# First context pair ahead of the loops' other work, and VectorE's last-stage weight work behind the row statistics

## The chip, the cores and the metric

One core of a Trainium2 chip runs the whole program. The time is device microseconds of one execution; three runs of the kernel before are shown, and one more execution was taken by the profiler. Engine names are the profile's: PE is TensorE, DVE VectorE, ACT ScalarE, POOL GpSimd, SP SyncE (which only issues transfers here).

## The reference

Two layers work on x of 64 batches x 128 rows x 256 columns in float32, each with cross attention to a context of the same shape and then a mixture of experts, all gated by tanh:

```python
x = x + tanh(g_xattn[0]) * xattn0(layernorm(x), ctx)      # 16 heads of 16, W_qkv, W_proj, b_proj
x = x + tanh(g_ffn[0])   * ffn0(layernorm(x))             # top 1 of 8 experts, capacity 1.5, 256-1024-256, gelu
x = x + tanh(g_xattn[1]) * xattn1(layernorm(x), ctx, ctx) # 16 heads of 16, wq, wk, wv, wo
x = x + tanh(g_ffn[1])   * ffn1(layernorm(x))             # top 2 of 4 experts, 256-256-256, two layer norms inside
```

In ffn0 every token is put into a slot of its expert's buffer (its place is the count of tokens before it with the same choice), the experts run over the slots, and each token reads its slot back, weighted with its softmax value.

## The kernel before

The work has four stages in a row. **The first attention loop** (n = 0) takes one batch of 128 rows per step through a pipeline that reaches over some 18 steps; step s works on batch s + 4 at one end (x_in is loaded) and on batch s - 12 at the other (its rows are scattered into the experts' slots in DRAM). **The expert stage** runs 39 groups of 256 slots through two layers, with weights split into a high and a low half. **The second attention loop** (n = 1) runs the same steps for layer 1; its input is x1 plus the weighted expert output, which an indirect DMA on GpSimd's queue gathers per batch (y_in, line 698, five steps ahead), and VectorE adds (x2 or "rows", line 1543, four steps ahead). **The last stage** (fstep) starts inside the tail of that loop.

Each engine has its own program, written out by hand: `step(s)` of that engine is a list of `if` blocks, each for one operation on its own batch, and the engine does them in the order of the text. Engines meet through counting semaphores. The attention loops are written out whole, with steps from -5 (LEAD) to 64 + 13 or 64 + 6, so "step 7" below is one definite place in each engine's program. The names that matter:

- Start of a loop. SyncE loads the weights (line 492), then in its steps x_in of batch s + 4 (line 529) and, in odd steps, the context c_t of the pair s + 3, s + 4 (line 536); for the first pair this is step -3, behind two x_in loads. In step -1 it waits until all four high and low halves of the key and value weights are made (s_wv, line 554) and loads the projection weights wp over w_vp (line 555). ScalarE makes wk_hi and wv_hi ahead of its steps (lines 818, 819), VectorE wv_lo and wk_lo (lines 1425, 1426), and TensorE waits for all four (line 1068).
- Context. ScalarE copies c_t to c_hi (line 861) and GpSimd subtracts to c_lo (line 730), both two steps ahead; TensorE makes the keys of a pair in one go (line 1148, 12 products; for the first pair in step -1), ScalarE copies them to k_in (line 869), and the values come a step later (line 1158). The values need wv_hi and wv_lo, the keys wk_hi and wk_lo.
- Rows. VectorE takes the statistics (bn_stats, bn_aggr, lines 1497, 1501, batch s + 3), GpSimd makes rstd (lines 675, 677), VectorE xh (line 1442), TensorE turns it (line 1216), ScalarE copies it to x_t (line 837), TensorE makes the query (line 1241).
- Scores. GpSimd masks k_in and q_in to km_r and qm (line 668); TensorE makes the scores of batch s - 1 (line 1098), VectorE their maximum nmax (line 1434, the first thing in its step, 2.29 us), TensorE turns it (line 1168), VectorE spreads it (nmax_x, line 1476), TensorE makes the final scores (lines 1075, 1081), ScalarE the exponential (line 889), TensorE the product with the values (line 1127). Then VectorE divides (rden, o_n, lines 1508, 1510), TensorE turns o_n in the next step (line 1111), ScalarE copies it (o_t, o_hi), GpSimd makes o_lo (line 714), TensorE projects (line 1227), and VectorE adds the residual (x1, line 1536).
- Weights of the last stage. SyncE loads them in step 2 of the second loop (line 490, 3 MB and some small ones). VectorE prepares them in 20 of the steps 7 to 42 (lines 1585 to 1652), at the end of its step, in pieces of mostly 1024 columns.
- Slots. In every fourth step of the first loop VectorE turns counts into slots (lines 1451 to 1470, for the chunk of four batches that begins with s - 12); GpSimd's scatters (line 740, batch s - 12) wait for them. The first group of the experts waits for the last scatter.
- End of the experts. SyncE stores the last block (line 590) and waits until it and the one before have landed (line 594) before it goes into the second loop; GpSimd waits for the same (line 753).

Of the kernel before, what the change touches and what calls it, by code (L numbers as in the profile page):

```python
# [5 lines left out]
P = 128  # L6
# [106 lines left out]
def flamingo_gated(nc, x, ctx_in, consts, gates, wq, wk, wv, wp, b_proj, router, w1_0, b1_0, w2_0, b2_0,  # L113
# [24 lines left out]
    QK_AT, PROB_AT = 11022, 15630  # L138
# [8 lines left out]
    with es:  # L147
# [58 lines left out]

        w_q = sb("w_q", [P, C, D])
# [23 lines left out]
        slot_in = psb("slot_in", [P, 4, 1], I32)  # L231
# [223 lines left out]
        def _(sp):  # L455
# [53 lines left out]
            for n in range(2):  # L509
# [8 lines left out]
                def step(s):  # L518
                    if n == 0 and s.known and s.off == FIRST_WEIGHTS:
                        weights(At(0, 0))  # L520
                    if n == 1 and s.known and s.off == LAST_WEIGHTS:
                        layer1_weights()
                    b = s + 4
# [6 lines left out]
                    e = s + 3  # L530
                    if e.off % 2 == 0 and e.within(B):
                        if (e - 3).begun:
                            sp.wait_ge(y["c_lo_done"].of(e - 3), y["c_lo_done"].at(e - 3))
                        for t in range(2):
                            b = e + t
                            sp.dma_start(c_t[:, e.off // 2 % 2, :, t, :], row(ctx_in, b).rearrange("p (c k) -> p c k", c=C))\
                                .then_inc(y["c_came"].of(b), 16)
# [22 lines left out]
                if n == 0:  # L560
# [32 lines left out]
                    for g in (NH - 2, NH - 1):  # L593
                        sp.wait_ge(z["eo_stored"].of(At(0, g)), z["eo_stored"].at(At(0, g)))
# [7 lines left out]
        def _(pool):  # L602
# [61 lines left out]
            for n in range(2):  # L664
# [14 lines left out]
                def step(s):  # L679
# [5 lines left out]
                    b = s - 5  # L685
                    if n == 0 and b.within(B):
                        if (b - 1).begun:
                            pool.wait_ge(y["xh2_done"].of(b - 1), y["xh2_done"].at(b - 1))
                        rstd(y["n2_stats"], mv2, rs2, y["n2_rstd"], b)
                    b = s + 5  # L690
                    if n == 1 and b.within(B):
# [17 lines left out]
                    b = s - 4  # L709
                    if b.within(B):  # L710
                        pool.wait_ge(y["o_t_done"].of(b), y["o_t_done"].at(b))
                        if (b - 2).begun:
                            pool.wait_ge(y["pr_done"].of(b - 2), y["pr_done"].at(b - 2))
                        nc.gpsimd.tensor_tensor(o_lo[:, b.parity], o_t[:, b.parity], o_hi[:, b.parity], ALU.subtract)\
                            .then_inc(y["o_lo_done"].sem, 1)
# [1111 lines left out]
```

## Time and profile before

| what | value |
|---|---|
| three runs | 2114.24, 2115.59, 2116.48 us (median 2115.59) |
| profiled execution | 2114.74 us |
| its span (first to last instruction) | 2112.6 us |
| mean granted TensorE clock | 0.985 |
| PE / DVE / ACT / POOL busy | 2019.0 / 1760.6 / 1479.2 / 1201.8 us |
| attention 0, experts, attention 1 and last stage | about 0 to 559, 559 to 1024, 1024 to 2113 us |

The profiled execution's own time is 2.1 us over its span. Busy shares are averages over stages with different limits; what one place is worth has to be read from the rows of that place. In the rows, times are microseconds from the start of the span; a row gives the start, the duration, the engine, the line, the operation, output<-inputs, and in square brackets how long the engine had been idle before it and what released it.

### The profile page before, as it was taken

Reading aid. Unit: us, or ns where it says so; the run is one execution under the profiler, and the core shown is the slowest. Engines: PE = TensorE matmul, PEld = TensorE weight load, DVE = VectorE, ACT = ScalarE, POOL = GpSimd, SP = SyncE. Lnnn points to the kernel's source line nnn. Section 1 sums busy time; section 2 is a strip of 40 time slices with the busy share of each in tenths; the row PEclk is TensorE's granted clock in tenths of the full one; section 3 lists DMA queues with packets and bytes.
Section 4 is the critical chain, followed back from the end, with each engine's and each line's share of the span. In section 5 each row is a group of like instructions: output and inputs, shape, how many; then the busy total and the mean of one; then the engine's idle time right before and its main releaser. Section 6 shows DMA issues by size and latency. Waiting matters only on the chain.

```text
span 2112.6 us, 57359 instructions
## 1 busy us (share of the span) xinstructions
PE 2019.0 (96%) x19532; PEld 1772.0 (84%) x19532; DVE 1760.6 (83%) x4918; ACT 1479.2 (70%) x3172; POOL 1201.8 (57%) x1736
## 2 busy tenths in 40 slices
PE   6999999999699999999699999999999999999997
PEld 5878888887599999999578887888788888888885
DVE  5888888888588888888588888888589999999996
ACT  4766666666487878787366666666578888888885
POOL 5778888887200000000377777777357777777776
PEclk9999999999799999999899999999999999999998
DMA  7565222221466666666422222222101100011000
GB/s 243 171 198 169 69 72 64 69 74 38 162 244 222 245 228 239 229 235 238 153 59 76 69 74 69 74 69 77 39 24 31 31 31 30 31 31 30 30 27 18
DMA packets 168047, 226.09 MB, mean 107 GB/s; under 512 B 20454, under 2 KB 152170, under 8 KB 157420
## 3 DMA queue, kind: packets, MB, share of 16 engines
q1 hardware_dynamic: 161644, 205.99, 29.5%
q0 software_dynamic: 6144, 16.79, 2.6%
q8 instruction: 145, 2.38, 0.5%
q14 instruction: 114, 0.93, 0.2%
HBM read 153.77 MB, written 68.94 MB: 105 GB/s over the span
## 4 chain that ended last, share of the span: by engine, by line
PE 87%; DVE 5%; issue 3%; DMA 2%; POOL 1%; ACT 1%; SPq 0%; POOLq 0%; ACTq 0%; DVEq 0%
PE ps L1281 11%; PE ps L1297 11%; PE ps L1041 10%; PE ps L1000 8%; PE ps L1081 5%; PE ps L1127 5%; PE ps L1241 4%; PE ps L1227 4%; PE ps L1148 4%; PE ps L1158 3%; PE ps L1181 3%; DVE nmax L1434 3%; PE ps L1060 3%; PE ps L1075 2%; PE ps L1098 2%
## 5 line engine op out<-in xcount | busy, mean ns | idle before, releaser
L1434 DVE TENSOR_REDUCE nmax<-ps 128x16 f32<-128x2048 f32 x128 | 292.8, 2287 | 32.6 <-PE ps L1098 32.2
L889 ACT ACTIVATE prob_t<-ps 128x2048 f32<-128x2048 f32 x128 | 240.8, 1881 | 102.4 <-PE ps L1081 102.4
L694 POOL COPY slot_in<-slot_all 128x1 int32<-128x1 int32 x64 | 13.3, 207 | 473.4 <-DMA eo_d<-eo 473.4
L1041 PE MATMUL ps<-w2f,a_t 128*128 128x256 f32 x1024 | 231.7, 379 | 0.3 <-ACT a_t L811 0.3
L1281 PE MATMUL ps<-xgt_hi,w_hl 128*128 128x256 f32 x1248 | 230.6, 283 | 1.0 <-DVE xgt_lo L1701 1.0
L1297 PE MATMUL ps<-w_hl,hid_hi 128*128 128x256 f32 x1248 | 226.9, 284 | 0.0
L1041 PEld LDWEIGHTS ps<-w2f,a_t 128*128 128x128 f32 x1024 | 189.6, 190 | 23.8 <-ACT a_t L811 0.6
L961 ACT ACTIVATE hid<-ps,b_in 128x256 f32<-128x256 f32 x312 | 145.8, 468 | 83.5 <-PE ps L1281 68.0
L1281 PEld LDWEIGHTS ps<-xgt_hi,w_hl 128*128 128x128 f32 x1248 | 196.0, 190 | 1.4 <-issue 1.4
L811 ACT ACTIVATE a_t<-ps,be_in,g_in 128x128 f32<-128x128 f32 x512 | 185.6, 469 | 12.3 <-PE ps L1060 11.4
L1297 PEld LDWEIGHTS ps<-w_hl,hid_hi 128*128 128x128 f32 x1248 | 191.5, 188 | 0.0
L1692 DVE TENSOR_TENSOR w_hl<-w_raw,w_hl 128x1024 fp32r<-128x1024 f32 x152 | 176.0, 1220 | 15.7 <-ACT w_hl L937 15.7
L668 POOL TENSOR_TENSOR km_r<-k_in,cst 128x512 fp32r<-128x512 f32 x128 | 134.4, 1050 | 96.0 <-ACT k_in L869 95.9
L1281 PE MATMUL ps<-xgt_lo,w_hl 128*128 128x256 f32 x624 | 176.6, 283 | 0.0
L1297 PE MATMUL ps<-w_hl,hid_lo 128*128 128x256 f32 x624 | 175.6, 281 | 0.0
L1717 DVE TENSOR_TENSOR hid_lo<-hid,hid_hi 128x256 fp32r<-128x256 f32 x312 | 132.5, 426 | 48.6 <-ACT hid_hi L967 42.5
L937 ACT ACTIVATE w_hl<-w_raw 128x1024 fp32r<-128x1024 f32 x152 | 148.2, 1057 | 0.0
L668 POOL TENSOR_TENSOR qm<-q_in,cst 128x512 f32<-128x512 f32 x128 | 133.5, 1043 | 20.3 <-PE ps L1081 17.6
L1127 PE MATMUL ps<-prob_t,v_aug 128*32 128x128 f32 x4096 | 138.4, 276 | 1.4 <-DVE x L1536 1.0
L1241 PE MATMUL ps<-x_t,w_q 128*128 128x128 f32 x1024 | 137.6, 278 | 0.8 <-ACT k_in L869 0.8
L1081 PE MATMUL ps<-qm,k_in 32*128 32x256 f32 x2048 | 132.1, 373 | 0.0
L1241 PEld LDWEIGHTS ps<-x_t,w_q 128*128 128x128 f32 x1024 | 127.5, 194 | 1.6 <-issue 1.6
(237 smaller groups left out, 6306.8 us busy)
## 6 DMA issues: line engine op xcount, KB each, us to landing
w_raw<-in_w_dram SPq DMA_DIRECT2D x78, 1024.0 KB, 6.8
c_t<-in_ctx_in_dram SPq DMA_DIRECT2D x128, 128.0 KB, 3.4
x_d<-x SPq DMA_DIRECT2D x128, 128.0 KB, 1.7
slots_d<-zeros SPq DMA_DIRECT2D x12, 1024.0 KB, 5.5
eo_d<-zeros SPq DMA_DIRECT2D x12, 1024.0 KB, 5.2
xg<-slots_d SPq DMA_DIRECT2D x39, 256.0 KB, 2.8
eo_d<-eo SPq DMA_DIRECT2D x39, 256.0 KB, 2.2
x_in<-in_x_dram SPq DMA_DIRECT2D x64, 128.0 KB
```

What stands on the lines that cost most here:

```text
L668: return nc.gpsimd.tensor_tensor(dst, src.unsqueeze(2).to_broadcast([P, 2, 2, P]), head_mask.unsqueeze(1).unsqueeze(3).to_broadcast([P, 2, ...
L811: nc.scalar.activation(a_t[:, b.parity, e, c, :], ps[:, 4 + e // 2, (e % 2 * 2 + c) * P:(e % 2 * 2 + c + 1) * P], ACT.Relu, scale=g1_in[:, ...
L889: nc.scalar.activation(prob_t[:].rearrange("p a k -> p (a k)"), scores.rearrange("p a k -> p (a k)"), ACT.Exp, scale=SOFT).then_inc(y["exp ...
L1000: mm = pe.matmul(dst, xt[:, b.parity, c, :], w[:, c, two, :].rearrange("p e n -> p (e n)"), start=(c == 0 and w is w1_hi and xt is xft_hi) ...
L1041: mm = pe.matmul(dst, a_t[:, b.parity, e, c, :], w2f[:, e, c, :], start=False, stop=True, skip_group_check=True)
L1081: mm = pe.matmul(scores[:, j, hf * 256:(hf + 1) * 256], k_in[r0:r0 + 32, b.off // 2 % 2, hf, b.off % 2, :], qm[r0:r0 + 32, p, hf, :, :].re ...
L1127: mm = pe.matmul(b6[32 * g:32 * g + 32, j * P:(j + 1) * P], v_aug[:, b.off % 4, h, :], prob_t[:, r, :], start=True, stop=True, tile_positi ...
L1241: mm = pe.matmul(b5[:, m * P:(m + 1) * P], w_q[:, c, m * P:(m + 1) * P], x_t[:, c, :], start=(c == 0), stop=(c == C - 1))
L1281: mm = pe.matmul(ps[:, 2 + fc % 4, 0:G], w_hl[:, q, w, at:at + P], xt[:, q, c, :], start=(k == 0), stop=(k == 5))
L1297: mm = pe.matmul(ps[:, q, i * D:(i + 1) * D], ht[:, fc, i * P:(i + 1) * P], w_hl[:, q, w, at:at + D], start=(fc == 0 and i == 0 and k == 0 ...
L1434: nc.vector.tensor_reduce(nmax[:, b.parity, :, 0:4], scores.rearrange("p a (r k) -> p a r k", k=P), AX_X, ALU.max, negate=True).then_inc(y ...
L1692: nc.vector.tensor_tensor(w_hl[:, g.parity, 1, cols], w_raws[g.parity][:, cols], w_hl[:, g.parity, 0, cols], ALU.subtract).then_inc(z["wl_ ...
```

## The change

All parts keep what is computed.

- In both loops the first pair's context is loaded in step -5, ahead of x_in; c_hi and c_lo of that pair are made in step -5 too, its keys and k_in in step -3 (before: c_t in -3, c_hi and c_lo in -2, keys in -1). In every step SyncE now issues the context ahead of x_in.
- ScalarE makes only wk_hi ahead of its steps; wv_hi comes at the end of step -2, VectorE's wv_lo in step -2 behind the row statistics. TensorE waits for the two key halves at the start, and for the value halves before the first values.
- SyncE no longer waits for the last two expert blocks to land; GpSimd does so only before its first gather, behind the copy of the slot numbers. For this slot_in gets memory of its own (two offsets move by 4 words).
- In the first loop's step 67, the last one with an o_lo, GpSimd makes o_lo ahead of the second rstd. The slots of the chunk that begins with batch 56 are made in step 67, not 68.
- In the second loop VectorE's 20 pieces of weight work come behind bn_aggr and ahead of rden, not at the step's end.

```diff
@@ sync
-                    b = s + 4
-                    if b.within(B):
-                        ...
-                        sp.dma_start(x_in[:, b.off % 12, :], row(x_src, b)).then_inc(y["x_came"].of(b), 16)
-                    e = s + 3
-                    if e.off % 2 == 0 and e.within(B):
+                    e = At(0, 0) if s.off == -LEAD else s + 3
+                    if (s.off == -LEAD or e.off > 0) and e.off % 2 == 0 and e.within(B):
                         if (e - 3).begun:
                             sp.wait_ge(y["c_lo_done"].of(e - 3), y["c_lo_done"].at(e - 3))
                         for t in range(2):
...
+                    b = s + 4
+                    if b.within(B):
...
+                        sp.dma_start(x_in[:, b.off % 12, :], row(x_src, b)).then_inc(y["x_came"].of(b), 16)
...
-                    for g in (NH - 2, NH - 1):
-                        sp.wait_ge(z["eo_stored"].of(At(0, g)), z["eo_stored"].at(At(0, g)))
@@ gpsimd
+                    def low_part():
+                        b = s - 4
...
+                    if (s - 4).within(B) and not (s - 3).within(B):
+                        low_part()
+                        second_rstd()
+                    else:
+                        second_rstd()
                     b = s + 5
                     if n == 1 and b.within(B):
...
+                        if b.off == 0:
+                            for g in (NH - 2, NH - 1):
+                                pool.wait_ge(z["eo_stored"].of(At(0, g)), z["eo_stored"].at(At(0, g)))
...
+                    if not ((s - 4).within(B) and not (s - 3).within(B)):
+                        low_part()
...
-                    e = s + 2
-                    if e.off % 2 == 0 and e.within(B):
+                    e = At(0, 0) if s.off == -LEAD else s + 2
+                    if (s.off == -LEAD or e.off > 0) and e.off % 2 == 0 and e.within(B):
@@ scalar
                 nc.scalar.activation(wk_hi[:], w_k[:], ACT.Copy).then_inc(s_wv[n], 1)
-                nc.scalar.activation(wv_hi[:], w_vp[:], ACT.Copy).then_inc(s_wv[n], 1)
...
-                    e = s + 1 if s.off == -1 else s
+                    e = At(0, 0) if s.off == -3 else s
...
+                    if s.off == -2:
+                        act.wait_ge(s_wv[n], 2)
+                        nc.scalar.activation(wv_hi[:], w_vp[:], ACT.Copy).then_inc(s_wv[n], 1)
@@ tensor
-                pe.wait_ge(s_wv[n], 4)
+                pe.wait_ge(s_wv[n], 2)
...
                     e = s - 1
                     if e.off % 2 == 0 and e.within(B):
+                        if e.off == 0:
+                            pe.wait_ge(s_wv[n], 4)
@@ vector
-                dve.wait_ge(s_wv[n], 2)
-                nc.vector.tensor_tensor(wv_lo[:], w_vp[:], wv_hi[:], ALU.subtract).then_inc(s_wv[n], 1)
+                dve.wait_ge(s_wv[n], 1)
                 nc.vector.tensor_tensor(wk_lo[:], w_k[:], wk_hi[:], ALU.subtract).then_inc(s_wv[n], 1)
...
-                    if n == 0 and b.off % CH == 0 and b.within(B):
+                    if n == 0 and b.off % CH == 0 and b.within(B) and b.off != B - 2 * CH:
+                        slots_from_places(b)
                     b = s - 11
...
+                        if b.off == B - 2 * CH:
+                            slots_from_places(b)
...
                         nc.vector.bn_aggr(mv1[:], st1[:]).then_inc(y["n1_stats"].sem, 1)
...
                     if n == 1 and s.off == LAST_SPLIT:
...
+                    if s.off == -2:
+                        dve.wait_ge(s_wv[n], 3)
+                        nc.vector.tensor_tensor(wv_lo[:], w_vp[:], wv_hi[:], ALU.subtract).then_inc(s_wv[n], 1)
+                    b = s - 3
+                    if b.within(B):
+                        dve.wait_ge(y["o1_done"].of(b), y["o1_done"].at(b))
...
```

## Rows read from the trace of the kernel before

**Rows 1.** The page: busy time, share of the span and instructions of an engine
```profile
PE 2019.0 (96%) x19532; PEld 1772.0 (84%) x19532; DVE 1760.6 (83%) x4918; ACT 1479.2 (70%) x3172; POOL 1201.8 (57%) x1736
```

**Rows 2.** Timeline of the start (start, duration, engine, line, operation, idle before)
```profile
9.48 0.63 ACT L861 ACTIVATE c_hi<-c_t 128x512 fp32r<-128x512 f32 x1
...
10.80 0.33 SPq L555 DMA_DIRECT2D w_vp<-in_wp_dram  x1
...
16.86 1.54 SPq L536 DMA_DIRECT2D c_t<-in_ctx_in_dram  x2
...
17.83 1.97 PE L1241 MATMUL ps<-x_t,w_q 128*128 128x128 f32 x8 [0.41 <-ACT k_in L869]
...
28.41 0.64 ACT L861 ACTIVATE c_hi<-c_t 128x512 fp32r<-128x512 f32 x1
```

**Rows 3.** Chain of waits, start: the key products
```profile
14.43 2.57 PE ps L1148 x12
```

**Rows 4.** Context loads issued at 26.0 to 28.0: from issue to landing
```profile
DMA to landing us min/median/max: 5.1/5.5/5.9
```

**Rows 5.** Timelines of the hand-over to the experts
```profile
538.76 0.58 PE L1227 MATMUL ps<-wp_hi,o_hi 128*128 128x256 f32 x1 [0.62 <-POOL o_lo L714]
...
548.70 0.15 DVE L1469 TENSOR_TENSOR slot_s<-slot_f,far 128x4 int32<-128x4 f32 x1
```

**Rows 6.** Timeline of the start of the second loop
```profile
1025.67 0.37 SPq L590 DMA_DIRECT2D eo_d<-eo  x1
...
1028.74 1.23 SPq L536 DMA_DIRECT2D c_t<-in_ctx_in_dram  x2
...
1033.20 0.63 ACT L861 ACTIVATE c_hi<-c_t 128x512 fp32r<-128x512 f32 x1 [12.75 <-DMA c_t<-in_ctx_in_dram]
...
1042.27 1.76 PE L1241 MATMUL ps<-x_t,w_q 128*128 128x128 f32 x8 [0.41 <-ACT k_in L869]
...
1047.43 0.56 DVE L1543 SCALAR_TENSOR_TENSOR rows<-y_in,wgt_all,x_in 128x256 f32<-128x256 f32 x1 [4.07 <-DMA y_in<-eo_d,slot_in]
...
1047.91 2.28 DVE L1434 TENSOR_REDUCE nmax<-ps 128x16 f32<-128x2048 f32 x1
...
1050.12 2.86 DVE L1442 TENSOR_SCALAR xh<-rows,mv,rs 128x256 f32<-128x256 f32 x1
...
1056.78 2.29 DVE L1434 TENSOR_REDUCE nmax<-ps 128x16 f32<-128x2048 f32 x1 [2.27 <-PE ps L1098]
```

**Rows 7.** Chain of waits there: two gathers (start, duration, what)
```profile
1031.12 3.96 DMA y_in<-eo_d,slot_in
...
1040.39 6.95 DMA y_in<-eo_d,slot_in
```

**Rows 8.** Timelines of VectorE: maxima of steps 7, 44 and 61
```profile
1092.16 2.29 DVE L1434 TENSOR_REDUCE nmax<-ps 128x16 f32<-128x2048 f32 x1
...
1368.35 2.29 DVE L1434 TENSOR_REDUCE nmax<-ps 128x16 f32<-128x2048 f32 x1 [0.47 <-PE ps L1098]
...
1491.28 2.29 DVE L1434 TENSOR_REDUCE nmax<-ps 128x16 f32<-128x2048 f32 x1 [0.99 <-PE ps L1098]
```

**Rows 9.** Timeline of steps 6 and 7, VectorE and GpSimd
```profile
1091.21 0.95 DVE L1543 SCALAR_TENSOR_TENSOR rows<-y_in,wgt_all,x_in 128x256 f32<-128x256 f32 x1
...
1096.63 1.04 POOL L668 TENSOR_TENSOR qm<-q_in,cst 128x512 f32<-128x512 f32 x1
...
1097.03 0.26 DVE L1508 RECIPROCAL rden<-ps 128x16 f32<-128x16 f32 x1 [0.64 <-PE ps L1181]
...
1098.82 1.22 DVE L1587 TENSOR_TENSOR w1f<-w1f,w_first 128x1024 f32<-128x1024 f32 x1
...
1099.96 2.28 DVE L1434 TENSOR_REDUCE nmax<-ps 128x16 f32<-128x2048 f32 x1
```

**Rows 10.** Timelines of step 30, GpSimd and VectorE
```profile
1268.16 1.27 POOL L730 TENSOR_TENSOR c_lo<-c_t,c_hi 128x512 fp32r<-128x512 f32 x1
...
1270.77 2.28 DVE L1434 TENSOR_REDUCE nmax<-ps 128x16 f32<-128x2048 f32 x1
```

More of the change, by code:

```diff
@@ L522, in step @@
                         layer1_weights()
+                    e = At(0, 0) if s.off == -LEAD else s + 3
+                    if (s.off == -LEAD or e.off > 0) and e.off % 2 == 0 and e.within(B):
+                        if (e - 3).begun:
+                            sp.wait_ge(y["c_lo_done"].of(e - 3), y["c_lo_done"].at(e - 3))
+                        for t in range(2):
+                            b = e + t
+                            sp.dma_start(c_t[:, e.off // 2 % 2, :, t, :], row(ctx_in, b).rearrange("p (c k) -> p c k", c=C))\
+                                .then_inc(y["c_came"].of(b), 16)
                     b = s + 4
@@ L684, in step, with second_rstd @@
                         rstd(y["n1_stats"], mv1, rs1, y["n1_rstd"], b)
[L685 to L689, printed above, removed]
+                    def second_rstd():
+                        b = s - 5
+                        if n == 0 and b.within(B):
+                            if (b - 1).begun:
+                                pool.wait_ge(y["xh2_done"].of(b - 1), y["xh2_done"].at(b - 1))
+                            rstd(y["n2_stats"], mv2, rs2, y["n2_rstd"], b)
+                    def low_part():
+                        b = s - 4
+                        if b.within(B):
+                            pool.wait_ge(y["o_t_done"].of(b), y["o_t_done"].at(b))
+                            if (b - 2).begun:
+                                pool.wait_ge(y["pr_done"].of(b - 2), y["pr_done"].at(b - 2))
+                            nc.gpsimd.tensor_tensor(o_lo[:, b.parity], o_t[:, b.parity], o_hi[:, b.parity], ALU.subtract)\
+                                .then_inc(y["o_lo_done"].sem, 1)
+                    if (s - 4).within(B) and not (s - 3).within(B):
[3 more added lines that the diff above has]
+                        second_rstd()
                     b = s + 5
@@ L853, in step @@
                         nc.scalar.activation(o_pad[:].rearrange("p a k -> p (a k)"), b6, ACT.Copy).then_inc(y["o_pad_done"].sem, 1)
-                    e = s + 2
-                    if e.off % 2 == 0 and e.within(B):
+                    e = At(0, 0) if s.off == -LEAD else s + 2
+                    if (s.off == -LEAD or e.off > 0) and e.off % 2 == 0 and e.within(B):
                         r = e.off // 2 % 3
@@ L1140, in step @@
                         pe.wait_ge(y["q_out"].of(s), y["q_out"].at(s))
-                    e = s + 1 if s.off == -1 else s
+                    e = At(0, 0) if s.off == -3 else s
                     if s.off != 0 and e.off % 2 == 0 and e.within(B):
@@ new lines, in step @@
+                    if n == 1 and s.off == LAST_SPLIT + 8:
+                        dve.wait_ge(s_fset2, 5)
+                        nc.vector.tensor_tensor(w1f[:, 0], w1f[:, 0], w1_mean[:, 0].unsqueeze(2).to_broadcast([P, E1, D]), ALU.subtract)\
+                            .then_inc(s_fset2, 1)
+                    if n == 1 and s.off == LAST_SPLIT + 10:
+                        nc.vector.tensor_tensor(w1f[:, 1], w1f[:, 1], w1_mean[:, 1].unsqueeze(2).to_broadcast([P, E1, D]), ALU.subtract)\
+                            .then_inc(s_fset2, 1)
```

148 lines of the change are left out of this document (64 added, 84 removed).

## Prediction

> **What bounds the kernel now.** I read the page first. TensorE is busy 96% of the span [rows 1], so in the steady stretches only fewer matmuls would help, and the change removes none. What it can reach are the places where TensorE stands still; I looked for them in the chain of waits and then in the timelines. There are four: the start of the program, the hand-over from the first loop to the experts, the start of the second loop, and those steps of the second loop in which VectorE prepares the last stage's weights.
>
> **Start of the program.** TensorE's first key product begins only after the first normalized rows are turned; the first query product follows at 17.83 [rows 2]. Ahead of it ScalarE makes both high weight halves and then the context's (c_hi at 9.48), and GpSimd's c_lo (1.27 us) starts only behind rstd [rows 2].
> New order: c_t is issued first, c_hi comes one ScalarE place of 0.6 earlier and ends near 9.4, c_lo runs to 10.7, and TensorE makes its 12 key products at once, 2.9 us as now (2.57 of them on the chain [rows 3]), from 10.85 to 13.8. k_in and wv_hi, 0.6 each as c_hi, end at 15.0, wv_lo, 0.7, at 15.7; then come the second xh (0.4), its turning, and the query product some 0.3 behind that turning's start, at 16.6. Gain 17.83 - 16.6 = **1.2**. Bounds: 0.3 (c_t or the later x_in lands a microsecond late) and 1.9. The price: SyncE's wait for four weight parts now lasts until 15.7, not 10.8, so the wp load (10.80 [rows 2]) and all behind it in that queue (x_in, the 2 MB of expert weights, the zero fills, the next c_t) move back 4.9 us. The context of batches 4 and 5, issued 16.86 to 18.40 [rows 2], would be issued by 23.3 and land about 28 (landing took 5.1 to 5.9 us in this crowded stretch [rows 4]); ScalarE wants it at 28.41 [rows 2] minus 1.2. That may cost ScalarE up to 2 us, but what it makes next, k_in, has over 1 us in hand before its exponential, so I cost it at nothing, with the lower bound above for it.
>
> **Hand-over to the experts.** In step 67 GpSimd makes rstd first and then o_lo of the last batch; TensorE's projection stands 0.62 us for it, from the end of the router product [rows 5]. With o_lo ahead of rstd that wait goes: 0.6. The slots of the last but one chunk move a step ahead (eight operations of some 0.1 us each in a row); they fit on VectorE before x1. The four scatters of that chunk then start about 2 us earlier, but the fifth, which goes 1.05 us behind the last chunk's slots now (slot_s at 548.70 [rows 5]), needs those slots, and those come through x1, statistics, rstd and router, which gain only the 0.6. So **0.6** in all, between 0 and 1.3.
>
> **Start of the second loop.** SyncE stores the last expert block at 1025.67, waits for its landing, and issues x_in and, at 1028.74, c_t; c_hi follows 4.4 us behind, at 1033.20, c_lo only behind four gathers, the query product at 1042.27 [rows 6]. After the change only GpSimd waits for the store. c_t is issued at 1026.1 and, with the same delay, a little less for the x_in loads that now come behind it, c_hi starts near 1030.2, c_lo 1030.9 to 1032.15, the key products to 1035.3. But GpSimd takes c_lo before its second gather and stands 1 us for it: gather 1 goes from 1031.12 [rows 7] to 1033.2, and with 2.05 us for each further gather (slot copy, 0.81 of issue, 1.09) and 0.85 for each rstd I get gather 4 at 1041.2 (now 1040.39 [rows 7]), km_r of batch 0 at 1045.3, 0.9 later than now, the first scores at 1046.4, as now: no gain so far, GpSimd is the bound.
> The gain comes next. Now VectorE waits 4.07 us for gather 4, which took 6.95 us because the last stage's 3 MB were issued just before it (gather 1 took 3.96) [rows 7], so the first maximum starts at 1047.91; then xh stands 2.86 us while GpSimd runs a gather and both masked products, and nmax_x starts at 1052.89, the next maximum at 1056.78 [rows 6]. In the new order SyncE's wait for wv_lo holds those 3 MB until 1042.2, behind gather 4, which I let land in 4.2 us, near gather 1's: x2 by 1045.9, maximum at 1046.95. Its rstd ends at 1049.45, xh runs at 1049.5 in the gap ahead of the gather, nmax_x at 1049.95, the turning and the queries to 1052.1, km_r to 1052.55, scores 0.5, second maximum at 1053.15: **3.6** gained. Bounds: 4.3 (km_r earlier), and -0.7 if gather 4 still takes 6.95.
>
> **Weight preparation.** From the maximum at 1092.16 to the one at 1368.35 are 37 steps, 276.19 us; the next 17 take 122.93, 7.231 each [rows 8]. The excess is 276.19 - 37 x 7.231 = **8.6 us**, for 20 steps that carry such work. In a step, VectorE is idle 0.64 us ahead of rden; a 1.22 us operation at the step's end pushes the maximum instead (1098.82, maximum at 1099.96 where the scores ended at 1099.26) [rows 9]. Behind the row statistics it costs rden 0.6, o_n and x1 0.4 (o_n ends 1098.4; TensorE turns it at 1099.2), and the maximum comes back to within 0.1 of the scores.
> But GpSimd's km_r and qm run there back to back (qm to 1097.67 [rows 9]), and in even steps c_lo behind them. Where VectorE reads two SBUF operands beside such work it waits: rows<- takes 0.95 instead of 0.49 beside c_lo, and gets the port when c_lo ends, ahead of GpSimd's next [rows 9]. So: five reductions (steps 10, 11, 24, 25, 27) have one operand and gain all. Five two-operand subtractions in odd steps wait 0.3 for km_r, push qm by 1.07, and gain all. Six in even steps push qm and, through it, c_lo to 1270.5 in the step of [rows 10]; rows<-, issued at 1269.55, waits for c_lo and the maximum starts at 1270.83, now 1270.77: nothing gained. The two long tensor_scalars (steps 36, 40) are even too: nothing. The step pairs that gain are worth (from the intervals between maxima) 0.27 x 4 for steps 7, 15, 17, 21, 1.09 for 9 to 12, 1.06 for 24 and 25, 0.25 for 27: **3.5**. Bounds: 8.6, all of it; and -11, the third rival.
> The Trainium skill, SBUF — State Buffer, section on the two separate sides, has this as an exclusive lock: the one that starts first keeps the shared port for its whole instruction, also against a VectorE operation with two SBUF inputs. The stretched rows agree. Without such a lock the even steps would gain as well, some 4.5 us more, and the time would be 2102; with it, 2106.7.
>
> **Sum.** 1.2 + 0.6 + 3.6 + 3.5 = 8.9 us. The profiled execution took 2114.74 (span 2112.6, 2.1 around it); it lies 0.85 under the median of the runs, 2115.59. 2114.74 - 8.9 = 2105.8 for it, **2106.7** against the median. A measurement of this kernel tells about 0.2%, 4.2 us, from no change.
>
> **Rivals.**
> First: the gathers, pushed behind c_lo, meet the weights after all. For: gather 4 took 6.95 us beside them [rows 7], and my gather 4 leads the weights by 1 us only. Then the first maximum is 0.7 late and xh is caught again: second loop -0.7 instead of 3.6, total 4.6, 2111.0. Chance 0.24.
> Second: the change does not do what it says in the weight steps: rden, being late, makes something else late (x1, the next o_lo), the excess stays, and the start of the second loop gives 0.5 since GpSimd's serial gathers pace it. 1.2 + 0.6 + 0.5 = 2.3, 2113.3. Against it: 0.8 us between o_n and its turning. Chance 0.13.
> Third, slower: VectorE, waiting at km_r, does not get the port between it and qm. For: the xh of 2.86 us let two such hand-overs pass [rows 6]. Against: rows<- got it ahead of GpSimd's next operation [rows 9], and does so in every even step. Odd: start at qm's end 1097.67, done 1098.75, 1.65 more of rden to rows<-, maximum 1100.4, 0.5 later than now, times 5. Even, subtractions and tensor_scalars: start at c_lo's end 1269.43, maximum 1272.15, 1.4 later, times 8. 2.5 + 11.2 = 13.7, less 2.4 of the reductions and 5.4 of the other parts: +5.9, 2121.5. It decides once eight of the thirteen lose: each costs 1.05 on average, and there are 7.8 to use up. Chance 0.07.
>
> **Numbers.** My forecast has 0.56. The range 2102.5 to 2113.5 takes in the upper bounds of the parts (1.9 + 0.8 + 4.3 + 6) and the first two rivals. Faster by over 0.2%: the forecast but for a little, and a little over half of the first rival, 0.70; within 0.2%: 0.24; slower: 0.06.
>
> **What would show it.** First query product near 16.6; c_lo of the second loop by 1032.5 relative to the store at 1025.7, gather 1 after it; second maximum 27.5 us after that store (now 31.1); odd weight steps near 7.23, even ones still 8.3 in places; qm after a subtraction late by 1.07. A two-operand subtraction of over 2 us, or a first maximum later than 22.2 us after the store, would make the prediction wrong.

## The result, and the profile after

The changed kernel took 2121.61 us (median of seven runs, 2120.97 to 2123.17) beside 2114.51 of the kernel before (seven runs, 2114.17 to 2116.48): ratio 1.0028, with a 95% interval of 1.0019 to 1.0038 (in brackets behind each ratio below). It is slower, and the interval is clear of no change. A second measurement beside 13 runs of the kernel before gave 1.0030 (1.0018 to 1.0041). The forecast was 2106.7.

The page of the kernel after, which answers to [rows 1]:
```profile
span 2119.3 us, 57372 instructions
PE 2024.0 (96%) x19532; PEld 1775.5 (84%) x19532; DVE 1800.3 (85%) x4918; ACT 1479.9 (70%) x3172; POOL 1204.6 (57%) x1736
```
The span grew by 6.7 us, and VectorE is busy 39.7 us longer with the same 4918 instructions. No work was added, so some of its instructions take longer: VectorE waits inside them.

To find where, I cut every profile at the starts of VectorE's row maxima (64 in each attention loop, counted here from 0; the one that the prediction calls step 7's is number 6) and at two marks of the expert stage: its first turning of gathered slots on TensorE, and its last pair of adds on VectorE. Microseconds of each stretch; "place as before" gives the profiles of experiments that have the old order there (how many in brackets; the experts and the tail are alike in all). In the fifth stretch that is, in the main, the order of the loop's start; six of its eight have the weight piece of step 7 in its new place.
```
stretch                                before   changed  again    place as before
start to maximum 4 of loop 1            49.11    48.32    49.34   47.56 to 49.52 (5)
maximum 4 to 63 of loop 1              470.63   481.96   481.92   471.73
maximum 63 to the experts' 1st turning  39.14    38.57    38.54   38.49 to 39.38 (5)
1st turning to the last expert add     465.30   464.41   464.36   464.46 to 465.56 (15)
last add to maximum 7 of loop 2         75.78    76.39    76.54   75.88 to 77.08 (8)
maximum 7 to 44                        275.64   271.27   271.29   275.56 to 275.60 (3)
maximum 44 to the end                  737.00   738.38   738.31   735.75 to 738.36 (15)
```
**Where the time went.** Loop 1 lost 11.3 us, in a stretch for which the prediction had no term at all. The weight preparation gained 4.4. All other stretches moved by less than they move between kernels with the same order there. The row before last begins behind step 7, which holds the first weight piece. With the cut in front of that step, at maximum 6, the start of loop 2 lost 1.2 us (67.98 to 69.18) and the weights gained 4.65 (276.19 to 271.54 from maximum 6 to 43).

The loop's middle, VectorE and then GpSimd, in a step with a slots block. First the kernel before (start, duration, engine, line, operation):
```profile
428.04 0.16 DVE L1457 TENSOR_SCALAR kept<-pos 128x4 f32<-128x4 f32 x1
...
428.31 0.17 DVE L1462 TENSOR_SCALAR far<-kept 128x4 f32<-128x4 f32 x1
...
428.66 0.16 DVE L1469 TENSOR_TENSOR slot_s<-slot_f,far 128x4 int32<-128x4 f32 x1
428.85 0.69 DVE L1476 TENSOR_TENSOR nmax_x<-ps,cst 128x512 fp32r<-128x512 f32 x1
```
The same block in the kernel after, VectorE:
```profile
435.73 0.69 DVE L1487 TENSOR_TENSOR nmax_x<-ps,cst 128x512 fp32r<-128x512 f32 x1 [0.26 <-PE ps L1182]
436.34 0.16 DVE L1468 TENSOR_SCALAR kept<-pos 128x4 f32<-128x4 f32 x1
...
436.60 0.89 DVE L1473 TENSOR_SCALAR far<-kept 128x4 f32<-128x4 f32 x1
437.41 0.15 DVE L1474 TENSOR_TENSOR slot_f<-ecap,posc 128x4 f32<-128x4 f32 x1
437.48 1.00 DVE L1476 SCALAR_TENSOR_TENSOR wgt_all<-p,g_t,kept 128x4 f32<-128x4 f32 x1
438.41 0.16 DVE L1479 CAST slot_all<-slot_f 128x4 int32<-128x4 f32 x1
438.48 1.23 DVE L1480 TENSOR_TENSOR slot_s<-slot_f,far 128x4 int32<-128x4 f32 x1
...
440.31 0.24 DVE L1596 RECIPROCAL rden<-ps 128x16 f32<-128x16 f32 x1
```
and GpSimd beside it:
```profile
436.41 1.06 POOL L666 TENSOR_TENSOR km_r<-k_in,cst 128x512 fp32r<-128x512 f32 x1 [1.72 <-ACT k_in L878]
437.43 1.03 POOL L666 TENSOR_TENSOR qm<-q_in,cst 128x512 f32<-128x512 f32 x1
438.43 1.26 POOL L742 TENSOR_TENSOR c_lo<-c_t,c_hi 128x512 fp32r<-128x512 f32 x1
```
The block's eight operations, 4 elements a partition each, ran from 428.04 to 428.82 before. Now they stand behind nmax_x, where GpSimd makes km_r, qm and c_lo back to back, and far ends with km_r (437.49 and 437.47), wgt_all with qm, slot_s with c_lo: 3.4 us for 0.8 us of work. Of the sixteen blocks thirteen took 3.10 to 3.47 us like this (0.78 before, and 2.37 for the first); the last three stand in steps in which GpSimd makes no km_r and qm, and took 0.78 to 1.03. rden and o_n wait behind them, and TensorE for o_n. The waits from 90 to 550 us (what waited, for what, total, times, longest), kernel after; neither row stands in the answer for the kernel before:
```profile
PEld ps L1123 <- DVE o_n L1598: 13.8, 13, 1.2
PE ps L1123 <- DVE o_n L1598: 11.1, 13, 1.0
```

### The profile page after: what moved, and what is told of

Same layout as the page of the kernel before. It is cut to its first block, busy times and chain, and to the rows that moved or that the text cites. A ratio compares the mean times of both kernels' runs of the same rounds, so it can differ in the third digit from the quotient of the medians.

```text
span 2119.3 us, 57372 instructions
## 1 busy us (share of the span) xinstructions
PE 2024.0 (96%) x19532; PEld 1775.5 (84%) x19532; DVE 1800.3 (85%) x4918; ACT 1479.9 (70%) x3172; POOL 1204.6 (57%) x1736
## 4 chain that ended last, share of the span: by engine, by line
PE 85%; DVE 7%; issue 4%; DMA 1%; POOL 1%; ACT 1%; SPq 0%; POOLq 0%; DVEq 0%; ACTq 0%
PE ps L1295 11%; PE ps L1311 10%; PE ps L1053 10%; PE ps L1012 8%; PE ps L1139 5%; PE ps L1160 4%; PE ps L1093 4%; PE ps L1255 4%; PE ps L1172 4%; PE ps L1241 3%; PE ps L1195 3%; PE ps L1072 3%; PE ps L1110 2%; PE ps L1087 2%; PE ps L1123 2%
## 5 line engine op out<-in xcount | busy, mean ns | idle before, releaser
L715 POOL DMA_INDIRECT y_in<-eo_d,slot_in x64 | 71.1, 1111 | 524.1 <-DMA eo_d<-eo 471.5
L821 ACT ACTIVATE a_t<-ps,be_in,g_in 128x128 f32<-128x128 f32 x512 | 185.6, 468 | 12.3 <-PE ps L1072 11.3
L666 POOL TENSOR_TENSOR qm<-q_in,cst 128x512 f32<-128x512 f32 x128 | 145.5, 1136 | 20.1 <-PE ps L1093 18.9
```

The lines of the kernel that those rows point to most:

```text
L666: return nc.gpsimd.tensor_tensor(dst, src.unsqueeze(2).to_broadcast([P, 2, 2, P]), head_mask.unsqueeze(1).unsqueeze(3).to_broadcast([P, 2, ...
L821: nc.scalar.activation(a_t[:, b.parity, e, c, :], ps[:, 4 + e // 2, (e % 2 * 2 + c) * P:(e % 2 * 2 + c + 1) * P], ACT.Relu, scale=g1_in[:, ...
```

## The experiments

Four sets; the kernels of one set ran on the same chip beside the same runs of the kernel before, so sets are compared by ratio and by the stretches of the profiles, not by raw medians.

### Whose 11 us: the slots block

One thing undone in the changed kernel:
```
+ b = s - 12                                  # ahead of nmax_x again
+ if n == 0 and b.off % CH == 0 and b.within(B) and b.off != B - 2 * CH:
+     slots_from_places(b)
  nmax_x ...
- (the same three lines behind nmax_x)
```


> The change with one thing undone: in the first loop the block that turns a chunk's places into slots (eight tiny VectorE operations, every fourth step) stands ahead of the row maximum nmax_x again; all else as changed. Theory L: behind the row maximum these tiny operations run into GpSimd's km_r, qm and c_lo and each waits a whole one of them; the loop lost about 11.4 us by it. Then this kernel takes 2121.6 - 11.4 = 2110.2 us (2109 to 2111.5), the block takes 0.8 us again, and the step of the row maxima in the middle of loop 1 keeps the offset it had at its start. Rival S: the loss sits in the start of loop 2 and the longer stretches; then this kernel stays within 2 us of 2121.6.


Measured: 2114.11 us (eleven runs, 2112.22 to 2116.28), 0.9992 (0.9983 to 1.0001), span 2112.3. Most of the loss is gone, so rival S is out, but the median lies above the 2109 to 2111.5 expected. Loop 1 gave back 7.3 us (474.67), not 11.4: counted from maximum 4 it is 3.3 us behind the kernel before at maximum 23 and 4.0 at 63. The fourth experiment below takes this up.

The same thing alone in the kernel before:


> The kernel before with that one thing done alone: the slots block behind the row maximum nmax_x, nothing else changed. Theory L: 2114.5 + 11.4 = 2125.9 us (2124 to 2128). Rival S: 2114.5, within 1.5 us. If the two pieces interact (the block collides only because the weights or the first pair also moved) it lands in between, and the first run says how much.


Measured: 2125.98 (2125.13 to 2127.19), 1.0047 (1.0034 to 1.0060); loop 1 took 482.50, 11.9 us more than before. The place of eight tiny operations is enough for the whole loss; nothing else of the change is needed.

Is it the overlap, or only that VectorE's queue is longer ahead of rden? The block stays behind nmax_x, but GpSimd doesn't start beside it:
```
+ c = s - 12                                  # GpSimd, ahead of km_r
+ if n == 0 and c.off % CH == 0 and c.within(B):
+     pool.wait_ge(y["slots_steps"].of(chunk(c)), y["slots_steps"].at(chunk(c)))
  pool.wait_ge(y["k_out"].of(b), y["k_out"].at(b)); masked(km_r ...)
```


> The change, with GpSimd made to wait in the steps that have a slots block until the block's steps are through, before its km_r; the block stays behind the row maximum. Theory L (the tiny operations wait for GpSimd's because both want the same access): without the overlap the block takes 0.8 us again, though km_r, qm and c_lo now start up to 1.7 us later; 2111 to 2115 us. Rival Q (the block costs by standing ahead of rden and o_n in VectorE's order, whatever runs beside it): the loss of 11 us stays or grows, 2121 to 2125 us.


Measured: 2118.22 (2114.09 to 2122.76, twelve runs), 1.0010 (0.9999 to 1.0020). The median lies between the two forecasts, and the executions scatter more than any other kernel's: five of the twelve took 2114.1 to 2115.1, the profiled one (2114.90) among them, and four 2121.9 to 2122.8. What follows is read from that one profile; what lengthens the longest four isn't known. Groups of instructions by line from 250 to 520 us (busy, mean ns), the changed kernel:
```profile
L1480 DVE TENSOR_TENSOR slot_s<-slot_f,far 128x4 int32<-128x4 f32 x8 | 8.8, 1100 | 0.0
L1476 DVE SCALAR_TENSOR_TENSOR wgt_all<-p,g_t,kept 128x4 f32<-128x4 f32 x8 | 8.3, 1033 | 0.0
L1473 DVE TENSOR_SCALAR far<-kept 128x4 f32<-128x4 f32 x8 | 7.2, 902 | 0.0
L1479 DVE CAST slot_all<-slot_f 128x4 int32<-128x4 f32 x8 | 1.2, 156 | 0.0
```
and this one:
```profile
L1479 DVE SCALAR_TENSOR_TENSOR wgt_all<-p,g_t,kept 128x4 f32<-128x4 f32 x8 | 1.7, 216 | 0.0
L1476 DVE TENSOR_SCALAR far<-kept 128x4 f32<-128x4 f32 x8 | 1.4, 170 | 0.0
L1483 DVE TENSOR_TENSOR slot_s<-slot_f,far 128x4 int32<-128x4 f32 x8 | 1.2, 156 | 0.0
```
In the same place in VectorE's order, without GpSimd beside them, the three take 156 to 216 ns again, and from maximum 28 to 63 the loop took 277.4 us (276.4 before, 285.2 in the changed kernel), although GpSimd's three operations now start behind the block. So in this execution the block stands as far ahead of rden as in the changed kernel and costs 1.0 us where it cost 8.8: its place in the queue doesn't explain the loss, the overlap does. This agrees with the Trainium skill, SBUF — State Buffer, section on the two separate sides, where the shared pair of ports is an exclusive lock for a whole instruction. But kept and posc, tensor_scalars as far is, began as km_r began and took their 0.16, and slot_f, with two inputs, went through the same change as far, in 0.15: which operation pays is a matter of tenths.

### The waits of steps 11 to 24

With the block ahead of nmax_x, VectorE waits in the early steps for scatters that run beside the 1 MB stores of zeros. Waits from 90 to 245 us of the first experiment, then of the kernel before:
```profile
DVE rows L1462 <- DMA slots_d<-rows,slot_s: 6.8, 4, 3.3
```
```profile
DVE rows L1449 <- DMA slots_d<-rows,slot_s: 6.9, 4, 2.6
```
So these waits are not new, and they are no reason for the first experiment to be 3 us behind the kernel before. With the block behind nmax_x this wait was 0.7 to 1.1 us in all, in three profiles. To get rid of it I divided the block: behind nmax_x for the first four chunks, ahead of it from the fifth.


> The change, with the slots block behind the row maximum nmax_x only for the first four chunks (steps 12 to 24, beside the stores of zeros) and ahead of it from the fifth chunk on. With the block behind it throughout, loop 1 had an offset of +0.5 us against the kernel before at step 24 and +10.5 at step 63; with it ahead throughout, +2.9 and +3.6, because in steps 11 to 24 VectorE then waited four times up to 3.3 us for the scatter of rows. Theory L with that side effect: the offset stays near +0.5 to +1 from step 28 on, so 2121.6 - 9.8 = 2111.8 us, and some 2 us below the run with the block ahead throughout. Rival: those waits are chance and not tied to the block's place; then the same as the run with the block ahead, 2114 us.


Measured: 2111.16 (2108.56 to 2112.96), 0.9974 (0.9963 to 0.9985); loop 1 in 471.53 us, 3.1 less than with the block ahead throughout. As expected. In the kernel before alone it was worth nothing:


> The kernel before with the slots block behind the row maximum for the first four chunks alone, nothing else changed. Its waits for the scatter of rows in steps 11 to 24 (9.8 and 10.2 us steps where 8 would do) go; the block costs 1.2 us a chunk behind the maximum. Theory: loop 1 from row maxima 4 to 63 takes 471.4 us, against 470.6 and 471.7 in the two profiles with the old place and 474.7 in one: 0 to 1.5 us faster than before and a smaller scatter between runs, ratio 0.9993 to 1.000. Rival (the place gains in itself, and the changed kernel's advantage needs nothing else): ratio below 0.999.


Measured: 2115.14, 1.0002 (0.9993 to 1.0011), loop 1 472.13. The old waits and the block's collisions cost about the same. Why the first experiment lost 3 us stays open. The change's own order (context loads ahead of the rows') doesn't explain it: the kernel with all edges and the block ahead (below) took 472.25. With the block ahead, four kernels took 470.6 (the kernel before), 471.7 (its loop 1 to the letter, in the run with the weights alone), 472.3 and 474.7 (the first experiment). The first part of the difference comes by maximum 14, behind the first slots block: 1.2, 1.1 and 2.4 us against the kernel before.

### The starts of the loops

The divided kernel, with loop 2's first context back in its old place (the new conditions only for n == 0):


> The run above, with the second loop's first pair of context back where it was before (loaded at step -3, c_lo behind the first gathers). First rival of the prediction (c_lo pushes the gathers to where the weights' load meets the fourth): the start of loop 2, from the last add of the expert stage to step 7, takes 1.2 to 1.8 us less, 2110.0 to 2110.6 us. If the start of loop 2 lost its time by anything else (the load of weights alone, the order of the row maxima): within 0.5 us of the run above.


Measured: 2110.62, 0.9973 (0.9963 to 0.9983). From the last add of the experts to the first maximum 23.92 us, not 24.65; to maximum 7 76.96, not 76.70. The first maximum does move by 0.7 as the first rival says (eight profiles with the old place: 23.73 to 24.02, and 24.19 in a ninth that has the context's load ahead of the rows' load; eight with the new: 24.32 to 24.75). Of this 0.54 us is still there at maximum 6 (68.92, not 69.46). Then step 7, with its weight piece, took 8.04 us for 7.24, and that is why maximum 7 comes later, not earlier. The 1.2 to 1.8 us expected up to there are not found, and the two medians differ by 0.5 us, which is within their intervals.

The weights' load two steps later (LAST_WEIGHTS 2 to 4, LAST_SPLIT 7 to 9), again on the divided kernel:


> The run with the divided slots block, with the load of the last stage's weights issued at step 4 of loop 2 and not at step 2, and the preparation two steps later as a whole. First rival (the fourth gather takes 7.2 us because the load runs beside it, and the row maximum of step 0 waits for it): the gather takes about 4 us and the start of loop 2 takes 2 to 3.6 us less, 2108.2 to 2110 us. If the gather is late by its own order and not by the load: 2111.8 us as above, and a later gather is the one that takes long.


Measured: 2110.99, 0.9975 (0.9964 to 0.9985): no gain. The first load of weights and the chain of waits in the kernel after, then the chain of this one:
```profile
1050.16 0.43 SPq L490 DMA_DIRECT2D w1f<-in_w_dram  x1
```
```profile
1050.17 7.21 DMA y_in<-eo_d,slot_in
1057.47 0.10 DVE rows L1631
```
```profile
1040.61 3.46 DMA y_in<-eo_d,slot_in
1044.15 2.70 DVE rows L1634
```
The gather landed in 3.46 us as expected. Then the row that uses it, on VectorE, and GpSimd beside it:
```profile
1044.15 4.05 DVE L1634 SCALAR_TENSOR_TENSOR rows<-y_in,wgt_all,x_in 128x256 f32<-128x256 f32 x1 [0.59 <-DMA y_in<-eo_d,slot_in]
...
1048.12 2.28 DVE L1447 TENSOR_REDUCE nmax<-ps 128x16 f32<-128x2048 f32 x1
```
```profile
1043.51 1.09 POOL L715 DMA_INDIRECT y_in<-eo_d,slot_in  x1 [0.80 <-POOL slot_in L708]
1044.63 1.05 POOL L666 TENSOR_TENSOR km_r<-k_in,cst 128x512 fp32r<-128x512 f32 x1
1045.63 1.05 POOL L666 TENSOR_TENSOR qm<-q_in,cst 128x512 f32<-128x512 f32 x1
1046.62 1.28 POOL L742 TENSOR_TENSOR c_lo<-c_t,c_hi 128x512 fp32r<-128x512 f32 x1
```
An operation of 0.48 us took 4.05 and ended 0.3 us behind c_lo, though it began ahead of km_r: two changes from one GpSimd operation to the next, and the one from the gather's issue to km_r, passed it over. What the earlier data gave, this wait took; only 0.4 us of the expected 2 to 3.6 were left at the first maximum.

All edges alone, slots and weights as before:


> The change's other half alone: the first pair's context first in both loops, wv_lo later, o_lo ahead at loop 1's end, GpSimd's wait for the last stores instead of SyncE's; slots block and weight preparation as before. By the ten profiles so far the stretches at the loops' ends and starts do not differ by more than their scatter between runs (start to row maxima 4: 47.6 to 49.1 us in three kernels with the old order, 48.0 to 49.3 in seven with the new; last row maxima of loop 1 to the experts' first transposes 38.5 to 39.1 against 38.5 to 38.8). Theory N (the edges are worth nothing): the same as the kernel before, ratio 0.999 to 1.001. The prediction's terms (1.2 + 0.6 + 3.6): 5.4 us faster, ratio 0.9975. First rival: 1.8 less 1.2 to 2 us, ratio about 1.000.


Measured: 2115.86 (eleven runs), 1.0008 (0.9998 to 1.0017). No gain of the edges together can be seen, and the 5.4 us of the prediction's terms are outside the interval. The times from start to maximum 4 overlap: 47.6 to 49.5 us in six profiles with the old order, 48.0 to 49.3 in eleven with the new.

### The hand-over to the experts

In the profile of that edges-only kernel the experts' first turning came 37.66 us after maximum 63, over 0.8 sooner than in any other profile until then. It is also the only one until then with o_lo early in which chunk 56's block had stayed in its step. Two runs to tell this from scatter, the divided kernel with odd pieces (below) with that block in its place, and the kernel before with divided slots, odd pieces and o_lo first:


> The run of odd pieces (divided slots block, all of the change's loop edges) with chunk 56's slots block back in its own step. In the profile with the edges alone, where the block had stayed, the experts' first transpose came 37.66 us after the last row maxima; with the block a step earlier it came 38.54 to 38.76 us after it in seven profiles, and the old order gives 38.5 to 39.1. Theory E (o_lo ahead gains 0.9 us, chunk 56's block then stands ahead of the logits of the next tile and takes 0.95 of it back): 37.7 us there, and 0.9 us less than the run of odd pieces in the profile, ratio 0.9955 to 0.9975. Rival (37.66 was chance): 38.6 us.

> The kernel before with divided slots and odd pieces, and o_lo ahead of the second statistics in loop 1's last step alone. Theory E: the experts' first transpose comes 37.7 us after the last row maxima and not 38.7; the whole 0.9 us less, ratio 0.9980 to 0.9985 with 0.9986 measured without it. Rival: 38.6 us and no difference.


Measured: 38.94 and 37.91 us; 2108.40 (2107.28 to 2108.99), 0.9963 (0.9949 to 0.9977), and 2109.08, 0.9969 (0.9956 to 0.9981). The second ratio is lower than the 0.9980 to 0.9985 expected, by more than the hand-over can give. As to the hand-over, one run is for theory E and one against. In the first, VectorE waited 1.07 us for a matmul ahead of the logits of a late tile, as in the kernel before (1.10); that wait is not in the other two kernels with o_lo early and the block in its step. Logits of that tile and the experts' turning, the changed kernel, then edges only:
```profile
550.30 0.16 DVE L1480 TENSOR_TENSOR slot_s<-slot_f,far 128x4 int32<-128x4 f32 x1
550.49 0.17 DVE L1615 COPY lg<-ps 128x8 f32<-128x8 f32 x1
...
568.85 1.09 PE L1276 MATMUL ps<-cst,xg 128*128 128x128 f32 x4 [11.68 <-DMA xg<-slots_d]
```
```profile
540.66 0.17 DVE L1545 COPY lg<-ps 128x8 f32<-128x8 f32 x1
...
559.09 1.09 PE L1276 MATMUL ps<-cst,xg 128*128 128x128 f32 x4 [11.74 <-DMA xg<-slots_d]
```
Relative to maximum 63 (530.28 and 521.43) the logits come at 20.21 and 19.23: in the changed kernel the block of chunk 56 stands right ahead of them and takes 0.98. So o_lo seems to gain some 0.9 where nothing else comes between, and the block that the change moved a step ahead takes it back; how often the wait of 1.07 takes the gain instead is open.

### The weights

> The kernel before with the second loop's weight preparation alone moved behind the row statistics. By the two traces steps 7 to 44 of loop 2 lost 4.65 us of length: 2114.5 - 4.7 = 2109.8 us (2108.5 to 2111.0), the steps with a two-operand piece at 8.1 us and the others near 7.2. Rival: the weights' gain comes only with the first pair's context moved, then within 1.5 us of 2114.5.


Measured: 2113.23 (eleven runs), 0.9989 (0.9980 to 0.9998); maximum 7 to 44 in 272.80 us for 275.64. The weights alone make the kernel before a little faster, by 2.8 us in that stretch and not the 4.65 expected (of 2114.5, 0.9989 makes 2112.2, not 2109.8). So the first pair's context isn't needed for a gain; what the stretch lacks beside the changed kernel stands in the pairs of steps that begin with 9, 17 and 21: 15.00, 14.97 and 15.92 us here, 14.44, 14.44 and 15.34 there.

Then the pieces moved one step on, from even steps to odd ones (LAST_SPLIT + 5, 15, 21, 23, 25, 27, 29, 31, 33, 35 each + 1), on the divided kernel:


> The run with the divided slots block, with each piece of the weight preparation that takes two operands from SBUF or is a tensor_scalar moved one step on, from an even step (in which GpSimd has c_lo beside km_r and qm) to the odd one. Theory L (what costs time is the wait for GpSimd's back-to-back operations, not the VectorE time): each of the six pieces that made a pair of steps 15.0 us instead of 14.46 costs nothing, 6 x 0.56 = 3.4 us less, 2108.4 us. Rival Q (the piece's own 0.6 to 1.4 us on VectorE is what the step lengthens by): same as with the pieces in even steps, 2111.8 us.


Measured: 2109.06 (2107.66 to 2110.67), 0.9965 (0.9953 to 0.9978); 270.00 us for 271.49: 1.5 gained, not 3.4. The same on the kernel before, without edges, and with loop 2's old context:


> The kernel before with the divided slots block and the weight preparation behind the row statistics with its pieces in odd steps: the run of odd pieces (2109.1 us, ratio 0.9965) without any change at the loops' edges. Theory N (the edges are worth nothing): ratio 0.996 to 0.997. If the edges are worth the prediction's 1.8 us or more beside this, it is 0.9975 or above.

> The run of odd pieces with the second loop's first pair of context back where it was. The same undoing gave 2110.6 for 2111.2 us with the pieces in even steps (ratios 0.9973 and 0.9974), where row maxima 0 came 0.7 us earlier after the last add of the expert stage and row maxima 7 0.3 us later. Theory N: the same as with the changed start, ratio 0.9960 to 0.9970. First rival in its own size (1.2 to 2 us): ratio 0.9955 to 0.9960.


Measured: 2111.48, 0.9986 (0.9977 to 0.9995), and 2110.95, 0.9983 (0.9974 to 0.9992); 271.88 and 271.62 us. Theory N had 0.9960 to 0.9970 for both, and missed; the first run even met the mark set for edges that are worth 1.8 us or more (0.9975 or above). Against that reading stand the edges-only kernel above and two kernels of the last set that have one edge each and ratios of 0.9971 and 0.9969; whether the edges are worth something beside pieces in odd steps stays open. Of the difference to the run with all edges 1.9 us lie in maximum 7 to 44. Two steps without a piece take 14.45 us. Thirteen pairs have a large piece in their odd step (7, 9, 15, 17, 21 and, moved, 23, 31, 33, 35, 37, 39, 41, 43). Of these ten took 14.95 to 15.04 in the first of the two runs, and in the run with all edges only six took more than 14.49. What differs can be seen in step 7. The subtraction of w1f there, in the changed kernel:
```profile
1105.90 1.05 POOL L666 TENSOR_TENSOR km_r<-k_in,cst 128x512 fp32r<-128x512 f32 x1
...
1106.59 1.45 DVE L1521 TENSOR_TENSOR w1f<-w1f,w_first 128x1024 f32<-128x1024 f32 x1
1106.89 2.04 POOL L666 TENSOR_TENSOR qm<-q_in,cst 128x512 f32<-128x512 f32 x1
```
and in the run with the weights alone:
```profile
1094.68 1.04 POOL L668 TENSOR_TENSOR km_r<-k_in,cst 128x512 fp32r<-128x512 f32 x1
...
1095.35 2.48 DVE L1504 TENSOR_TENSOR w1f<-w1f,w_first 128x1024 f32<-128x1024 f32 x1
1095.68 1.04 POOL L668 TENSOR_TENSOR qm<-q_in,cst 128x512 f32<-128x512 f32 x1
```
Above, the subtraction gets in between km_r and qm, and qm shows 2.04 for 1.04. Below, it stood waiting as long before km_r's end (just under 0.4 us), and qm went first; it took 2.48 us and the step 8.02, not 7.21. Is SyncE's order of two loads enough to turn this, and does the same program turn out the same again?


> The kernel before with divided slots and odd pieces (0.9986), and SyncE's order of the change in every step: the context's load ahead of the rows' load; no other edge. In loop 2 the pieces in odd steps cost 0.5 us a pair of steps in that run (14.95 us) and mostly nothing (14.45) in the run with all the edges. Theory R (who gets the access at the change from one GpSimd operation to the next is decided by small shifts, and this order is one of them): pairs at 14.45 us in five or more of eight, 7 to 44 of loop 2 in 270.0 us and not 271.9. Rival (the order of the loads has nothing to do with it): 271.9 us, the pairs at 14.95.

> The changed kernel once more, on the chip and beside the runs of the kernel before that the other three share, for a second profile. Ratio 1.002 to 1.004; loop 1 from row maxima 4 to 63 in 482 us (481.96 in the first), the block's wgt_all, far and slot_s near 1.0, 0.9 and 1.1 us each again; loop 2 from 7 to 44 in 271.3 to 272.5 us; hand-over 38.6 us. If the 0.5 us pairs in odd steps are a race without a rule, they will not all stand where the first profile has them.


Measured: 2109.58, 0.9971 (0.9958 to 0.9983), 270.48 us, with three of the eight moved pieces at 14.46 and not five, and five of the thirteen pairs where it was three without the order of loads: between the two theories. But the kernel with o_lo early, which has the old order of loads, shows nearly the same pattern (270.56, five pairs too), so the order of loads isn't needed for it. The changed kernel's second profile (2122.22; 1.0030, 1.0018 to 1.0041) repeats the first: loop 1 in 481.92, slot_s, wgt_all and far at 1102, 1035 and 900 ns, maximum 7 to 44 in 271.29, and the same pairs long. So the one program that was profiled twice kept its outcomes; programs with small differences elsewhere have others.

## Why the prediction was wrong

**The step that failed** stands in the hand-over: "the slots of the last but one chunk move a step ahead (eight operations of some 0.1 us each in a row)". The diff moves all sixteen chunks' blocks, fifteen of them from ahead of nmax_x to behind it in the same step, and I read only the sixteenth. So loop 1 had no term; it measured +11.3 (+10.2 beside the other profile with the old code of that loop), and the block's place alone makes it, as the second experiment shows (+11.9). The prediction itself had what was needed: GpSimd's back-to-back operations there, waits for the port, and the third rival's price of one pass. It applied them to the weights alone. That rival's time, 2121.5, is the measured one, but from another place than the one it names.

**Start of the program**, 1.2: nothing that can be told. The first query product came at 15.88, 1.9 earlier, earlier than the 16.6 I wrote; the first maximum came at 21.46 for 22.71, but at 22.70 in the second profile of the same kernel, and over six and eleven profiles no gain is left at maximum 4. The step that failed: carrying an early product through to the loop as a gain, from one profile, where equal starts scatter by 2 us from profile to profile.

**Hand-over**, 0.6: o_lo's term was right in kind in two of three experiments (37.66 and 37.91 us, where four of the six with the old order have 38.50 to 38.70); the chunk's block was costed at "they fit on VectorE before x1"; it stands ahead of the logits and takes 0.98 back.

**Start of loop 2**, 3.6: the first rival came true. The step that failed is the lead of 1 us that the fourth gather was to have over the weights: it was issued at 1050.17 and they at 1050.16. It took 7.21 us beside them and xh was caught for 2.59. The first maximum is 0.9 to 1.0 later; the second came 31.8 us after the store, where the kernel before has 31.1 and the prediction 27.5. But the lead would not have given the 3.6 either: with the gather at 3.46 us the next row waited for GpSimd instead, and only 0.4 was gained.

**Weight preparation**, 3.5: about right in size. In the prediction's own stretch 4.65 and 4.62 in the changed kernel's two profiles; from maximum 7 on 4.4 there, and 2.8 to 4.4 over six kernels with the pieces as the change has them. Steps with reductions and odd steps went to 7.20 to 7.26 as forecast (7.37 and 7.12 in one pair), the six even ones with a subtraction to 8.10 to 8.16 (8.30 to 8.52 before, but 7.79 in step 22), a little better than nothing gained. That an odd subtraction gets the port ahead of qm holds for this program and not for others.

**Sum.** Of the spans' 6.7 us, 11.3 are loop 1's slots and 0.6 loop 2 up to maximum 7, less 4.4 of the weights: 7.5. The other four stretches (0.8, 0.6 and 0.9 gained, 1.4 lost) are within what they scatter. The lower end of the range, 2102.5, was added up from 0.8 for the hand-over and 6 for the weights, where the working gives bounds of 1.3 and 8.6; what was missing stood at the other end, where no bound allowed for a loss in loop 1.

## What to carry to other kernels

When a diff turns a block into a function, follow every caller and write down for each queue what now stands where; a block of tenths of a microsecond deserves its line in the sum if it is moved across the start of another engine's work. Beside back-to-back GpSimd work an operation of VectorE with two SBUF operands, or a tensor_scalar, can cost what is left of the GpSimd operation, whatever its own size (far, wgt_all and slot_s did here, kept and slot_f did not): keep chains of tiny ones out of there. And judge edges from several profiles of both kernels, since one stretch scatters here by as much as an edge is worth.

The kernel that came out of this, all of the change with the divided block, the weight pieces in odd steps and chunk 56's block in its step, took 2108.40 us, 0.9963 (0.9949 to 0.9977) of the kernel before, and 13.8 us less than the changed kernel in the same set. Its ratio is the lowest of all variants here, though the ratios of six others lie within its interval.

## What the runs showed of the hardware

- The price of such a wait of VectorE's is set by GpSimd's instruction: operations on 4 elements a partition took 0.89, 1.00 and 1.23 us beside operations of 1.06, 1.03 and 1.26 us, and 0.17, 0.22 and 0.16 without.
- At the change from one GpSimd operation to the next, VectorE got in (far, wgt_all; w1f in 1.45) or was passed over (w1f in 2.48, rows in 4.05). Just under 0.4 us of waiting before the change stood before both outcomes. What decides is not settled; two profiles of one program agreed.
- An indirect gather of 128 rows landed in 3.46 us with nothing large ahead and in 6.6 to 7.2 beside 3 MB issued at about the same time; moving the load made this gather faster, not the kernel.
